# A's table on SyncE's queue, w0 indices in two reads, and the last stores cut differently in a low-rank-adapted residual kernel

## The chip, the cores and the metric

The kernel runs on one core of a Trainium2 chip. The metric is device microseconds of one execution, given as the median of several runs. Before the change it is 76.97 us (3 runs, 76.96 to 77.12). The engines are TensorE (PE), VectorE (DVE), ScalarE (ACT), GpSimd (POOL) and SyncE (SP), and 16 DMA engines move the data that the queues of SP, ACT and POOL issue.

## The reference, cut to what matters

```python
x = x + einsum('bct,bcd->bdt', x, L0_weights[cond])           # layer 0: 32 samples, 64x64 matrix each, picked from 200
H = einsum('btd,od->bto', x, W)                                # layer 1: 512 -> 512
xa = einsum('btd,brd->btr', x, A[adapter])                     # rank 16, picked from 8 adapters
delta = einsum('btr,bor->bto', xa, Bm[adapter]) * scalings[adapter][:, None, None]
out = x + H + delta
```

x is 32 samples of 64 x 512 in fp32.

## The kernel before, in words

Layer 1 works along the width and layer 0 along the channels, so the kernel multiplies by W plus the identity first (z), and applies layer 0, with the identity added to its matrices, to z afterwards. Two samples of 64 channels make one tile of 128 partitions, so there are 16 tiles (TILES = 16, 0 to 15). fp32 accuracy comes from splitting each operand in a high part (rounded to fp32r) and a low part (the difference), and adding three products; ACT makes the high parts and DVE the low ones. Tiles 0 and 1 (PLAIN = 2) are multiplied in plain fp32 instead, because they run before the split operands are there.

For a tile, PE computes z in two banks of 272 columns (`products`, L654; `plain_products`, L642, for tiles 0 and 1): the A part, which also holds the 32 columns of A (x times the adapter's A), and the W part. ACT and DVE take z out of PSUM in its high and low parts. `weigh_low_rank` (L688, L685) multiplies the low-rank columns by layer 0's matrix, `take_low_rank` (L540) and `low_of_low_rank` (L546) prepare them on DVE. `layer0` (L709, L710, L696, L714) then makes the output of the tile with four matmuls: two for z_high, one for the low-rank part with b, one for z_low. `take_out` (L413) copies it from PSUM to `out_sb` on ACT, and SP stores it.

All engines run a hand-written order and meet at semaphores. The PE order per tile is: A bank, two thirds of the W bank, layer 0 of the tile before, weigh_low_rank, last third of the W bank.

**The start.** The first transfers are index_sb, head_b, head_d and w_late on SP's queue (L241 to L244), and head_a, head_c and a_scales (A's table with the scalings, 260 KB) on ACT's (L327 to L329). SP then waits for the indices, reads those of layer 0's matrices of tiles 0 to 3 (8 values, `read_indices`), and issues the loads of these matrices (`load_w0`, L232, two DMAs of 16 KB a tile) with x of tile 3 between them (L228). From tile 4 on it reads four values at a time. POOL waits for a_scales (L306) before its first load of b (`load_b`, L290), then adds the identity to layer 0's matrices (`add_identity`, L299) and copies A's columns (`take_a`, L283), in this order: b of tiles 0 and 1, identity of tile 0, of tile 1, b of 2, A columns of 2, b of 3, identity of tiles 2 and 3, A columns of 3. ACT's `high_of_w0` (L400) and DVE's `low_of_w0` (L502) split layer 0's matrices of tiles 2 and 3 after that identity. On DVE `low_of_w0` stands ahead of `take_low_rank(2)` (L540).

**The end.** PE makes layer 0 of tile 14 whole (512 columns, `out_ps[0]`), then layer 0 of tile 15 in two parts: the A part (240 columns, `out_ps[1]`), then the W part (272 columns, a v_ps bank). ACT takes out tile 14 (L413), takes out tile 15's A part (L466) and issues its store (L469); SP stores tile 14 (L238); DVE takes out tile 15's W part (L629), and SP stores it (L265). ACT waits until all stores have landed (L471).

Of the kernel before, what the change touches and what calls it, by code (L numbers as in the profile page):

```python
# [6 lines left out]
def adapted_residual_kernel(nc, xt, heads, w0, head_a, head_b, head_c, head_d, w_late_t, a_t, b_t, out):  # L7
# [4 lines left out]
    ACT = mybir.ActivationFunctionType  # L12
# [5 lines left out]
    TILES = xt.shape[0] + EARLY  # L18
    C = w0.shape[1]
    PER = P // C  # L20
    K = WIDTH // P
    ADAPTERS, RANK, OUT = b_t.shape
# [9 lines left out]
    READ = 2  # L32
# [4 lines left out]
    AHEAD = 6  # L37
# [45 lines left out]
    with ctx:  # L83
# [6 lines left out]
        def sem(name):  # L90
            return ctx.enter_context(nc.semaphore(name))
# [9 lines left out]
        a_scales = sb("a_scales", [P, ADAPTERS * K * RANK + ADAPTERS], fp32)  # L101
# [19 lines left out]
        out_sb = sb("out_sb", [P, TILES, OUT], fp32)  # L121
# [9 lines left out]
        a_loaded = sem("a_loaded")  # L131
# [36 lines left out]
        z_low_ready = [sem("z_low_a_ready"), sem("z_low_w_ready")]  # L168
        out_done = sem("out_done")
        out_ready = sem("out_ready")  # L170
        last_done = sem("last_done")
        last_ready = sem("last_ready")
        stored = sem("stored")

# [30 lines left out]
        def read_indices(eng, kind, t, count, tiles):  # L205

            _, values = nc.values_load_multi_w_load_instructions(
                index_sb[0:1, PER * (TILES * kind + t):PER * (TILES * kind + t + tiles)], engines=(eng.engine,), min_val=0, max_val=count - 1)
            return [values[PER * i:PER * (i + 1)] for i in range(tiles)]
# [8 lines left out]
        def z_part(t, part):  # L218
            bank = bank_of(t, part)
            at, col, n = Z_PARTS[side(t)][bank]  # L220
            if t < PLAIN and part == A_PART and RAW_A[t] == 0:
                at += AC
            return z_ps[t % 2][:, bank, at:at + n], col, n

        @block.sync
        def _(sync):
            def load_x(t):
                sync.dma_start(x_raw[:, t - EARLY, :], xt[t - EARLY]).then_inc(x_loaded[t - 2], 16)  # L228

            def load_w0(which, t):  # L230
                for s in range(PER):
                    sync.dma_start(w0_sb[s * C:(s + 1) * C, t, s * C:(s + 1) * C],  # L232
                                   w0[ds(which[s], 1), :, :].rearrange("a c d -> (a c) d"),
                                   ).then_inc(w0_loaded[BATCH_OF[t]], 16)

            def store(t):
                sync.wait_ge(out_ready, t + 1)
                sync.dma_start(out[PER * t:PER * (t + 1), :, :].rearrange("s c l -> (s c) l"),  # L238
                               out_sb[:, t, :]).then_inc(stored, 16)

            sync.dma_start(index_sb[:], heads.rearrange("(a n) -> a n", a=1)).then_inc(index_loaded, 16)  # L241
            sync.dma_start(head[:, HEAD_AT[1]:HEAD_AT[2]], head_b).then_inc(head_loaded[1], 16)  # L242
            sync.dma_start(head[:, HEAD_AT[3]:HEAD_AT[4]], head_d).then_inc(head_loaded[3], 16)
            sync.dma_start(w_late[:, :, AC:AC + LATE], w_late_t).then_inc(w_late_loaded, 16)  # L244
            sync.wait_ge(index_loaded, 16)
            which = read_indices(sync, 0, 0, w0.shape[0], 2 * READ)
            sync.wait_ge(w0_cleared, 1)
            load_w0(which[0], 0)
            load_w0(which[1], 1)
            load_x(3)  # L250
            load_w0(which[2], 2)
            load_w0(which[3], 3)
            for t in range(4, TILES):
                if t % READ == 0:
                    which = read_indices(sync, 0, t, w0.shape[0], READ)
                load_x(t)
                load_w0(which[t % READ], t)
                if t >= AHEAD:
                    store(t - AHEAD)
            for t in range(TILES - AHEAD, TILES - 1):  # L260
                store(t)
            last = TILES - 1
            _, col, n = z_part(last, W_PART)
            sync.wait_ge(last_ready, 1)
            sync.dma_start(out[PER * last:, :, col:col + n].rearrange("s c l -> (s c) l"),  # L265
                           out_sb[:, last, col:col + n]).then_inc(stored, 16)

        @block.gpsimd
        def _(pool):
# [56 lines left out]
        def _(act):  # L326
            act.dma_start(head[:, HEAD_AT[0]:HEAD_AT[1]], head_a).then_inc(head_loaded[0], 16)  # L327
            act.dma_start(head[:, HEAD_AT[2]:HEAD_AT[3]], head_c).then_inc(head_loaded[2], 16)
            act.dma_start(a_scales[:], a_t).then_inc(a_loaded, 16)  # L329
            nc.scalar.activation(warmed[:], nc.const_aps.tensor(1.0, [1, 1], fp32), ACT.Copy)  # L330
            act.wait_ge(index_loaded, 16)
            first = read_indices(act, 1, 0, ADAPTERS, PLAIN)
# [78 lines left out]
            def take_out(t):  # L411
                act.wait_ge(out_done, t + 1)
                nc.scalar.activation(out_sb[:, t, :], out_ps[t % 2][:], ACT.Copy).then_inc(out_ready, 1)  # L413
# [31 lines left out]
            for t in range(3, last):  # L445
# [9 lines left out]
                if t % 2:  # L455
# [4 lines left out]
            high_of_z(last, A_PART)  # L460
            high_of_v(last)
            high_of_z(last, W_PART)
            take_out(last - 1)
            _, col, n = z_part(last, A_PART)
            act.wait_ge(out_done, last + 1)
            nc.scalar.activation(out_sb[:, last, col:col + n], out_ps[last % 2][:, 0:n],  # L466
                                 ACT.Copy).then_inc(out_ready, 1)
            act.wait_ge(out_ready, TILES)
            act.dma_start(out[PER * last:, :, col:col + n].rearrange("s c l -> (s c) l"),  # L469
                          out_sb[:, last, col:col + n]).then_inc(stored, 16)  # L470
            act.wait_ge(stored, 16 * (TILES + 1))  # L471

        @block.vector
        def _(dve):
# [149 lines left out]
            low_of_b(last)  # L624
            low_of_v(last)
            low_of_z(last, W_PART)
            _, col, n = z_part(last, W_PART)
            dve.wait_ge(last_done, 1)
            nc.vector.tensor_copy(out_sb[:, last, col:col + n], v_ps[(last + 1) % 2][:, 0:n]).then_inc(last_ready, 1)  # L629

        @block.tensor
        def _(pe):
# [72 lines left out]
            def layer0(t, dst, col, n, parts):  # L705
                pe.wait_ge(w0_low_ready, BATCH_OF[t] - BATCH_OF[PLAIN] + 1)
                for part in parts:
                    pe.wait_ge(z_high_ready[part], t - PLAIN + 1)
                nc.tensor.matmul(dst, w0_parts[:, t, 0, :], z_high[:, t % 2, col:col + n], start=True, stop=False)  # L709
                nc.tensor.matmul(dst, w0_parts[:, t, 1, :], z_high[:, t % 2, col:col + n], start=False, stop=False)  # L710
                add_low_rank(t, dst, col, n, False)
                for part in parts:
                    pe.wait_ge(z_low_ready[part], t - PLAIN + 1)
                return nc.tensor.matmul(dst, w0_parts[:, t, 0, :], z_low[:, t % 2, col:col + n], start=False, stop=True)  # L714

            def whole_layer0(t):
                pe.wait_ge(out_ready, t - 1)
                layer0(t, out_ps[t % 2][:], 0, OUT, (A_PART, W_PART)).then_inc(out_done, 1)
# [51 lines left out]
            w_bank(last, 0, 2 * K)  # L770
            weigh_low_rank(last)
            w_bank(last, 2 * K, 3 * K)
            whole_layer0(last - 1)
            pe.wait_ge(out_ready, last - 1)
            _, col, n = z_part(last, A_PART)
            layer0(last, out_ps[last % 2][:, 0:n], col, n, (A_PART,)).then_inc(out_done, 1)
# [52 lines left out]
```

## Time and profile before

| | |
|---|---|
| median of 3 runs | 76.97 us |
| the profiled execution's own time | 76.68 us |
| its span, first to last instruction | 75.0 us |
| granted TensorE clock | 1.000 of full speed in the mean |
| TensorE busy | 94% of the span |
| DVE, ACT, POOL busy | 74%, 68%, 44% |
| share of the chain that ended last | PE 86%, DMA 8% |
| DMA | 14.55 MB, mean 194 GB/s |

The times of the rows below are in microseconds from the span's start. A timeline row gives start, duration, engine, line, operation and what it writes and reads; in brackets stands how long the engine sat idle before it and what ended that. The chain of work that ended last is followed back from the last instruction and printed in order of time. In the names, SPq, ACTq and POOLq are the parts of these engines that issue DMAs. DMA queue q1 is SP's, q10 ACT's, q0 POOL's.

### The profile page before, as it was taken

To read this page: it belongs to the slowest core of one execution; us is meant where nothing else is said; L and a number is where in the kernel's file an instruction comes from. 1 tells how busy PE (TensorE), PEld (TensorE's weight loads), DVE (VectorE), ACT (ScalarE), POOL (GpSimd) and SP (SyncE) were. 2 spreads that over 40 slices of the span, in tenths; PEclk is the share of its full clock that TensorE was granted. 3 is DMA by queue.
4 is the path that set the end of the run, shared out by engine and by line. 5 is a ranking of instruction groups with operands and counts; after the bars stand their busy time and mean duration, and the time that the engine had idled before them with its cause. 6 is when DMAs were issued, how large, how long until landed. Compare 5 with 4: busy or idle time off the path is not lost.

```text
span 75.0 us, 1943 instructions
## 1 busy us (share of the span) xinstructions
PE 70.7 (94%) x468; PEld 65.4 (87%) x468; DVE 55.2 (74%) x143; ACT 51.3 (68%) x126; POOL 32.8 (44%) x76
## 2 busy tenths in 40 slices
PE   5999899999999999999999999999999999999940
PEld 5996689786999999999999999999999999999930
DVE  3019499897989877979797959797797949765920
ACT  0733888957988686977668666867696867566440
POOL 5700399997846282556245620690258320000000
PEclk9999999999999999999999999999999999999999
DMA  0999378786678757978968675578326430303025
GB/s 0 290 389 380 87 227 231 209 253 194 187 246 285 254 166 234 253 217 294 334 211 294 223 261 143 141 212 282 120 62 220 140 144 0 140 13 140 0 100 179
DMA packets 9677, 14.55 MB, mean 194 GB/s; under 512 B 3650, under 2 KB 4418, under 8 KB 9666
## 3 DMA queue, kind: packets, MB, share of 16 engines
q1 hardware_dynamic: 7554, 9.16, 37.5%
q0 software_dynamic: 1536, 4.20, 18.4%
q10 hardware_dynamic: 576, 1.07, 4.1%
q8 instruction: 4, 0.07, 0.4%
q14 instruction: 7, 0.06, 0.3%
HBM read 10.23 MB, written 4.19 MB: 192 GB/s over the span
## 4 chain that ended last, share of the span: by engine, by line
PE 86%; DMA 8%; SPq 1%; DVE 1%; issue 0%
PE z_ps L654 56%; DMA head<-head_d 8%; PE z_ps L642 6%; PE out_ps L696 5%; PE out_ps L709 4%; PE out_ps L710 4%; PE out_ps L714 4%; PE v_ps L688 2%; PE out_ps L702 2%; DVE out_sb L629 1%; PE v_ps L685 1%; SPq L242 0%; SPq L241 0%; PE v_ps L714 0%; PE v_ps L710 0%
## 5 line engine op out<-in xcount | busy, mean ns | idle before, releaser
L654 PE MATMUL z_ps<-moving,x_high 128*128 128x272 f32 x224 | 33.2, 288 | 0.0
L654 PEld LDWEIGHTS z_ps<-moving,x_high 128*128 128x128 f32 x224 | 29.8, 188 | 0.7 <-ACT z_plain L373 0.2
L290 POOL DMA_DIRECT2D b_raw<-b_t x32 | 16.2, 508 | 14.4 <-DMA a_scales<-a_t 5.4
L654 PE MATMUL z_ps<-moving,x_low 128*128 128x272 f32 x112 | 18.8, 289 | 0.0
L654 PEld LDWEIGHTS z_ps<-moving,x_low 128*128 128x128 f32 x112 | 15.8, 188 | 0.1
L511 DVE TENSOR_TENSOR z_low<-z_ps,z_high 128x272 fp32r<-128x272 f32 (+1 forms) x28 | 11.8, 422 | 1.2 <-ACT z_high L364 0.2
L283 POOL CAST moving<-a_table 128x128 fp32r x28 | 8.0, 316 | 10.5 <-PE z_ps L654 10.5
L520 DVE TENSOR_TENSOR b_stack<-b_raw,b_high 128x512 fp32r<-128x512 f32 x16 | 11.5, 718 | 0.4 <-ACT b_high L380 0.4
L380 ACT ACTIVATE b_high<-b_raw,group_sb 128x512 fp32r<-128x512 f32 x16 | 11.5, 716 | 0.0
L394 ACT ACTIVATE v_high<-v_ps,group_sb 128x128 fp32r<-128x128 f32 x16 | 5.9, 366 | 7.8 <-PE v_ps L688 7.8
L364 ACT ACTIVATE z_high<-z_ps 128x272 fp32r<-128x272 f32 (+1 forms) x28 | 10.5, 376 | 0.5 <-PE z_ps L654 0.3
L488 DVE TENSOR_TENSOR x_low<-x_raw,x_high 128x512 fp32r<-128x512 f32 x13 | 9.8, 757 | 0.1
L413 ACT ACTIVATE out_sb<-out_ps 128x512 f32<-128x512 f32 x15 | 8.8, 590 | 0.5 <-PE out_ps L714 0.5
L387 ACT ACTIVATE x_high<-x_raw 128x512 fp32r<-128x512 f32 x13 | 8.3, 637 | 0.0
L409 ACT ACTIVATE low_rank_parts<-own_low_rank 128x96 fp32r<-128x96 f32 x14 | 4.0, 284 | 5.9 <-DVE own_low_rank L540 5.9
L299 POOL TENSOR_TENSOR w_sb<-w_sb,ident 128x256 f32<-128x256 f32 (+1 forms) x9 | 6.9, 769 | 2.5 <-DMA w_sb<-w 2.4
L696 PE MATMUL out_ps<-b_stack,v_stack 128*128 128x512 f32 (+1 forms) x16 | 7.0, 435 | 0.0
L546 DVE TENSOR_TENSOR low_rank_parts<-own_low_rank,low_rank_parts 128x32 fp32r<-128x32 f32 x14 | 3.2, 227 | 4.9 <-ACT low_rank_parts L409 4.9
L709 PE MATMUL out_ps<-z_high,w_parts 128*128 128x512 f32 (+1 forms) x14 | 5.4, 388 | 0.0
L710 PE MATMUL out_ps<-z_high,w_parts 128*128 128x512 f32 (+1 forms) x14 | 5.4, 383 | 0.0
L714 PE MATMUL out_ps<-z_low,w_parts 128*128 128x512 f32 (+1 forms) x14 | 5.4, 382 | 0.0
L560 DVE SCALAR_TENSOR_TENSOR v_stack<-v_ps,group_sb,v_rest 128x128 fp32r<-128x128 f32 x14 | 4.9, 351 | 0.5
(58 smaller groups left out, 77.1 us busy)
## 6 DMA issues: line engine op xcount, KB each, us to landing
b_raw<-b_t POOLq DMA_DIRECT2D x32, 128.0 KB, 3.2
out<-out_sb SPq DMA_DIRECT2D x15, 256.0 KB, 3.2
x_raw<-xt SPq DMA_DIRECT2D x13, 256.0 KB, 3.7
w_sb<-w SPq DMA_DIRECT2D x32, 16.0 KB, 3.2
w_late<-w_late_t SPq DMA_DIRECT2D x1, 480.0 KB, 6.9
head<-head_c ACTq DMA_DIRECT2D x1, 400.0 KB, 4.2
head<-head_d SPq DMA_DIRECT2D x1, 384.0 KB, 6.1
head<-head_a ACTq DMA_DIRECT2D x1, 264.0 KB, 2.9
```

What stands on the lines that cost most here:

```text
L290: pool.dma_start(b_raw[s * C:(s + 1) * C, t % BBUFS, :], b_t[ds(which[s], 1), :, :].rearrange("a r (g n) -> (a r) g n", g=1) .to_broadcast ...
L364: nc.scalar.activation(z_high[:, t % 2, col:col + n], z, ACT.Copy).then_inc(z_high_ready[part], 1)
L380: nc.scalar.activation(b_high[:, t % 2, :], b_raw[:, t % BBUFS, :], ACT.Copy, scale=group_sb[:, LOW_B:LOW_B + 1]).then_inc(b_high_ready, 1)
L413: nc.scalar.activation(out_sb[:, t, :], out_ps[t % 2][:], ACT.Copy).then_inc(out_ready, 1)
L488: nc.vector.tensor_tensor(out=x_low[:, t % XBUFS, :], in0=x_of(t), in1=x_high[:, t % XBUFS, :].bitcast(fp32), op=ALU.subtract).then_inc(x_ ...
L511: nc.vector.tensor_tensor(out=z_low[:, t % 2, col:col + n], in0=z, in1=z_high[:, t % 2, col:col + n].bitcast(fp32), op=ALU.subtract).then_ ...
L520: nc.vector.tensor_tensor(out=b_stack[:, t % 2, :], in0=b_raw[:, t % BBUFS, :], in1=b_high[:, t % 2, :].bitcast(fp32), op=ALU.subtract).th ...
L654: last = nc.tensor.matmul(z_bank(t, part), x[:, t % XBUFS, k * P:(k + 1) * P], moving[:, int(n == HL), k, at:at + HALF], start=((n, k) == ...
L696: return nc.tensor.matmul(dst, v_stack[:, t % 2, :], b_stack[:, t % 2, col:col + n], start=False, stop=stop)
L709: nc.tensor.matmul(dst, w0_parts[:, t, 0, :], z_high[:, t % 2, col:col + n], start=True, stop=False)
L710: nc.tensor.matmul(dst, w0_parts[:, t, 1, :], z_high[:, t % 2, col:col + n], start=False, stop=False)
L714: return nc.tensor.matmul(dst, w0_parts[:, t, 0, :], z_low[:, t % 2, col:col + n], start=False, stop=True)
```

## The change

Four edits:

1. The load of a_scales moves from ACT's queue (third there) to SP's, between head_d and w_late.
2. The indices of layer 0's matrices for tiles 0 to 3 are read in two steps of four values instead of one of eight: the second step stands after x of tile 3 is issued.
3. Layer 0 of tile 14 is computed in two halves of 256 columns, the first into `out_ps`, the second into tile 14's own z bank, which is free by then. ACT takes each half out as it is done, and SP stores each by itself.
4. Of tile 15, DVE takes out the A part and SP stores it; ACT takes out the W part, the last one, and issues its store itself.

```diff
+            sync.dma_start(a_scales[:], a_t).then_inc(a_loaded, 16)
             sync.dma_start(w_late[:, :, AC:AC + LATE], w_late_t).then_inc(w_late_loaded, 16)
             sync.wait_ge(index_loaded, 16)
-            which = read_indices(sync, 0, 0, w0.shape[0], 2 * READ)
+            which = read_indices(sync, 0, 0, w0.shape[0], READ)
             sync.wait_ge(w0_cleared, 1)
             load_w0(which[0], 0)
             load_w0(which[1], 1)
             load_x(3)
-            load_w0(which[2], 2)
-            load_w0(which[3], 3)
+            which = read_indices(sync, 0, READ, w0.shape[0], READ)
+            load_w0(which[0], 2)
+            load_w0(which[1], 3)
...
-            _, col, n = z_part(last, W_PART)
-            sync.wait_ge(last_ready, 1)
-            sync.dma_start(out[PER * last:, :, col:col + n].rearrange("s c l -> (s c) l"),
-                           out_sb[:, last, col:col + n]).then_inc(stored, 16)
+            sync.wait_ge(half_ready, 1)
+            store_columns(last - 1, 0, OUT // 2)
+            sync.wait_ge(out_ready, last)
+            store_columns(last - 1, OUT // 2, OUT // 2)
+            _, col, n = z_part(last, A_PART)
+            sync.wait_ge(first_ready, 1)
+            store_columns(last, col, n)
...
-            act.dma_start(a_scales[:], a_t).then_inc(a_loaded, 16)
...
-            take_out(last - 1)
-            _, col, n = z_part(last, A_PART)
-            act.wait_ge(out_done, last + 1)
-            nc.scalar.activation(out_sb[:, last, col:col + n], out_ps[last % 2][:, 0:n],
+            act.wait_ge(half_done, 1)
+            nc.scalar.activation(out_sb[:, last - 1, 0:OUT // 2], out_ps[(last - 1) % 2][:, 0:OUT // 2],
+                                 ACT.Copy).then_inc(half_ready, 1)
+            act.wait_ge(out_done, last)
+            nc.scalar.activation(out_sb[:, last - 1, OUT // 2:], z_ps[(last - 1) % 2][:, 0, 0:OUT // 2],
                                  ACT.Copy).then_inc(out_ready, 1)
-            act.wait_ge(out_ready, TILES)
+            _, col, n = z_part(last, W_PART)
+            act.wait_ge(last_done, 1)
+            nc.scalar.activation(out_sb[:, last, col:col + n], v_ps[(last + 1) % 2][:, 0:n],
+                                 ACT.Copy).then_inc(last_ready, 1)
+            act.wait_ge(last_ready, 1)
             act.dma_start(out[PER * last:, :, col:col + n].rearrange("s c l -> (s c) l"),
                           out_sb[:, last, col:col + n]).then_inc(stored, 16)
...
-            _, col, n = z_part(last, W_PART)
-            dve.wait_ge(last_done, 1)
-            nc.vector.tensor_copy(out_sb[:, last, col:col + n], v_ps[(last + 1) % 2][:, 0:n]).then_inc(last_ready, 1)
+            _, col, n = z_part(last, A_PART)
+            dve.wait_ge(out_done, last + 1)
+            nc.vector.tensor_copy(out_sb[:, last, col:col + n], out_ps[last % 2][:, 0:n]).then_inc(first_ready, 1)
...
-            whole_layer0(last - 1)
+            pe.wait_ge(out_ready, last - 2)
+            layer0(last - 1, out_ps[(last - 1) % 2][:, 0:OUT // 2], 0, OUT // 2,
+                   (A_PART, W_PART)).then_inc(half_done, 1)
+            layer0(last - 1, z_ps[(last - 1) % 2][:, 0, 0:OUT // 2], OUT // 2, OUT // 2,
+                   (A_PART, W_PART)).then_inc(out_done, 1)
```

## Rows read from the trace of the kernel before

**Rows 1.** The chain in order of time: start, us, what
```profile
1.71 6.11 DMA head<-head_d
...
70.21 0.23 PE out_ps L709
...
71.14 0.11 PE out_ps L709
...
71.96 0.14 PE v_ps L714
...
72.12 0.44 DVE out_sb L629
```
**Rows 2.** Timeline of ACT and SP from 65 us on
```profile
71.18 0.60 ACT L413 ACTIVATE out_sb<-out_ps 128x512 f32<-128x512 f32 x1 [0.53 <-PE out_ps L714]
71.67 0.36 ACT L466 ACTIVATE out_sb<-out_ps 128x240 f32<-128x240 f32 x1
72.06 0.36 ACTq L469 DMA_DIRECT2D out<-out_sb  x1
...
72.59 0.33 SPq L265 DMA_DIRECT2D out<-out_sb  x1
```
**Rows 3.** DMA issues, us to landing: tile 13 (66 to 70 us), then tile 15's stores
```profile
out<-out_sb SPq DMA_DIRECT2D x1, 256.0 KB, 2.0
...
out<-out_sb SPq DMA_DIRECT2D x1, 136.0 KB, 2.0
out<-out_sb ACTq DMA_DIRECT2D x1, 120.0 KB, 2.2
```
**Rows 4.** DMA traffic in 73:73.3, 73.3:73.6 and 73.6:73.9 us, one row each
```profile
DMA packets 54, 0.11 MB, mean 369 GB/s; under 512 B 0, under 2 KB 0, under 8 KB 54
...
q10 hardware_dynamic: 83, 0.08, 81.6%
...
DMA packets 113, 0.10 MB, mean 333 GB/s; under 512 B 16, under 2 KB 113, under 8 KB 113
```
**Rows 5.** Start: issues to landing, ACT's issue of a_scales, q10 in 6.0:6.5 and 7.0:7.5
```profile
w_late<-w_late_t SPq DMA_DIRECT2D x1, 480.0 KB, 6.9
...
a_scales<-a_t ACTq DMA_DIRECT2D x1, 260.0 KB, 6.2
...
1.79 0.45 ACTq L329 DMA_DIRECT2D a_scales<-a_t  x1
...
q10 hardware_dynamic: 69, 0.13, 68.6%
...
q10 hardware_dynamic: 3, 0.00, 2.2%
```
**Rows 6.** Timelines of PE, POOL, ACT, DVE and PE's weight loads, 8 to 19 us
```profile
9.42 2.00 PE L642 MATMUL z_ps<-w_late,head 128*128 128x272 f32 x8
...
8.77 2.27 POOL L290 DMA_DIRECT2D b_raw<-b_t  x4 [5.41 <-DMA a_scales<-a_t]
...
14.90 1.06 POOL L299 TENSOR_TENSOR w_sb<-w_sb,ident 128x256 f32<-128x256 f32 x1
...
16.00 0.42 ACT L400 ACTIVATE w_parts<-w_sb 128x256 fp32r<-128x256 f32 x1 [0.82 <-POOL w_sb L299]
...
16.91 0.41 DVE L502 TENSOR_TENSOR w_parts<-w_sb,w_parts 128x256 fp32r<-128x256 f32 x1
17.33 0.19 DVE L540 TENSOR_TENSOR own_low_rank<-z_ps,own_rank 128x32 f32<-128x32 f32 x1
...
18.14 0.19 PEld L688 LDWEIGHTS v_ps<-w_parts,low_rank_parts 128*128 128x128 f32 x1 [0.39 <-DVE low_rank_parts L546]
```
**Rows 7.** SP's queue, 2 to 12 us; then landing of its last w0 issue of tile 3
```profile
2.18 0.67 SPq L244 DMA_DIRECT2D w_late<-w_late_t  x1
...
9.42 2.44 SPq L232 DMA_DIRECT2D w_sb<-w  x4
...
w_sb<-w SPq DMA_DIRECT2D x1, 16.0 KB, 3.3
```

More of the change, by code:

```diff
@@ L170, in adapted_residual_kernel @@
         out_ready = sem("out_ready")
+        half_done = sem("half_done")
+        half_ready = sem("half_ready")
         last_done = sem("last_done")
+        first_ready = sem("first_ready")
         last_ready = sem("last_ready")
@@ L259, in _, with store_columns @@
                     store(t - AHEAD)
-            for t in range(TILES - AHEAD, TILES - 1):
+            last = TILES - 1
+            for t in range(TILES - AHEAD, last - 1):
                 store(t)
-            last = TILES - 1
-            _, col, n = z_part(last, W_PART)
-            sync.wait_ge(last_ready, 1)
-            sync.dma_start(out[PER * last:, :, col:col + n].rearrange("s c l -> (s c) l"),
-                           out_sb[:, last, col:col + n]).then_inc(stored, 16)
+            def store_columns(t, col, n):
+                sync.dma_start(out[PER * t:PER * (t + 1), :, col:col + n].rearrange("s c l -> (s c) l"),
+                               out_sb[:, t, col:col + n]).then_inc(stored, 16)
+            sync.wait_ge(half_ready, 1)
[5 more added lines that the diff above has]
+            store_columns(last, col, n)
         @block.gpsimd
@@ L462, in _ @@
             high_of_z(last, W_PART)
-            take_out(last - 1)
-            _, col, n = z_part(last, A_PART)
-            act.wait_ge(out_done, last + 1)
-            nc.scalar.activation(out_sb[:, last, col:col + n], out_ps[last % 2][:, 0:n],
-                                 ACT.Copy).then_inc(out_ready, 1)
-            act.wait_ge(out_ready, TILES)
+            act.wait_ge(half_done, 1)
[3 more added lines that the diff above has]
+            nc.scalar.activation(out_sb[:, last - 1, OUT // 2:], z_ps[(last - 1) % 2][:, 0, 0:OUT // 2],
+                                 ACT.Copy).then_inc(out_ready, 1)
+            _, col, n = z_part(last, W_PART)
[3 more added lines that the diff above has]
+            act.wait_ge(last_ready, 1)
             act.dma_start(out[PER * last:, :, col:col + n].rearrange("s c l -> (s c) l"),
                           out_sb[:, last, col:col + n]).then_inc(stored, 16)
-            act.wait_ge(stored, 16 * (TILES + 1))
+            act.wait_ge(stored, 16 * (TILES + 2))
         @block.vector
```

## The prediction

> **What bounds the kernel now.** I read the chain that ended last first, in order of time. It begins with the landing of head_d at 1.71 + 6.11 = 7.82 us, runs through TensorE's matmuls without a gap worth naming up to 72.10 us, and leaves by DVE's copy of tile 15's W part, 72.12 + 0.44 = 72.56 us [rows 1]. So the kernel is TensorE's work plus a head and a tail, and an edit can win only in these two. The middle is touched only if the head lets TensorE begin it earlier.
>
> The tail next. SP issues the last store at 72.59 us [rows 2], it lands 2.0 us later [rows 3], at 74.59, and the span ends at 75.0: 0.4 us of closing work. Three stores are in flight there: tile 14's 256 KB, issued when ACT's copy of it is done (71.18 + 0.60 = 71.78), 120 KB issued by ACT at 72.06, 136 KB by SP at 72.59 [rows 2]. The reader is to see that they queue. Tile 13's 256 KB, with nothing beside it, took 2.0 us from issue to landing; the last store, with half the bytes, took 2.0 us too, and ACT's, still smaller, 2.2 [rows 3]. ACT's queue moves most of its bytes between 73.3 and 73.6 us, over 1.2 us after its issue at 72.06 [rows 2, 4].
>
> The head last. PE starts tile 0's A bank at 9.42 us; w_late, which it needs, lands at 2.18 + 6.9 = 9.08 [rows 5 to 7]. Behind that stands a second chain, which shares nothing with PE's. a_scales is issued on ACT's queue at 1.79 and lands 6.2 us later, at 7.99 [rows 5]. POOL, which had waited 5.41 us for it, starts its first b load at 8.77 and adds the identity to tiles 2 and 3 from 14.90 to 15.96 [rows 6]. ACT waits 0.82 us for this and splits these matrices at 16.00. DVE takes their low part at 16.91 to 17.32, starts `take_low_rank(2)` at 17.33, and PE's weight load for `weigh_low_rank(2)`, idle for 0.39 us, starts at 18.14 upon it [rows 6]. Whatever PE wins before 18.14 is lost there unless POOL is earlier too. This is the most important reading for the head.
>
> **The tail, part by part.** Tile 14 in halves: four matmuls of 512 columns take 4 x 0.23 us, those of 240 columns 0.11 each [rows 1], in proportion. Eight of 256 columns cost 8 x 0.115 = 0.92 us, what four cost now; the four extra weight loads are hidden as they are in tile 15's parts. Bounds: 0 to +0.1 us; I take 0. PE begins tile 14 at 70.21, so the first half is done at 70.67 and the second at 71.13. ACT's copies took 0.60 us for 512 columns and 0.36 for 240 [rows 2], so 0.37 for 256: 70.71 to 71.08 and 71.17 to 71.54. SP issues at 71.11 and 71.57. The A part leaves PE at 71.14 + 4 x 0.11 = 71.58. DVE's copy took 0.44 us for 272 columns [rows 1], so about 0.42 for 240, and SP issues at 72.05. SP is idle before each of these issues; an issue takes 0.33 us there [rows 2], so none stands in another's way. The W part leaves PE at 72.10. ACT copies 272 columns in 0.36 to 0.44 us (its own 240, DVE's 272), I take 0.40, and issues at 72.55 to 72.58, against 72.59 now: the hand-over itself wins 0.02 us.
>
> What wins is the queue. With 2 KB rows the engines moved 369 GB/s, with rows of about 1 KB 333 [rows 4]. Tile 13's 0.262 MB took 0.71 us of its 2.0 by the first rate, so 1.29 us are fixed. A half of tile 14 (0.131 MB) then moves in 0.39 us, the A part in 0.37, the W part (0.139 MB) in 0.42. The issues are 0.46, 0.48 and 0.52 us apart, each more than the transfer before it needs, so nothing is left in the queue when the last begins. It lands 1.29 + 0.42 = 1.71 us after 72.57, at 74.28, where it was 74.59: -0.31 us. Bounds: -0.40 if the small stores also move at the higher rate and the copy is at its short end, +0.18 if a store issued by ACT needs 2.2 us here too.
>
> The Trainium skill speaks against this edit: "DMA: Bandwidth & Descriptors" gives, under "Anatomy of one DMA", a fit of about 2.0 us plus bytes / 436 GB/s, and under "Rules for kernel authors" it wants small transfers joined. By that fit, an estimate from the page for another issue path, the last store would need 2.32 us and land at 74.89, and the sum would be +0.30. The trace disagrees: tile 13's store needed 2.0 us where the fit gives 2.60.
>
> **The head, part by part.** a_scales on SP's queue: its issue takes the place of w_late's, 2.18 in place of 1.79, but its bytes move far later, most of them around 6.0 to 6.5, and the last three packets after 7.0 [rows 5]. The order of issue, a, b, c, d, a_scales, w_late, stays what it was. head_d no longer shares with it and may land up to 0.5 us earlier; but PE then waits for w_late, whose bytes stand behind the same sum as before and which lands at 9.08. PE could start at about 9.25 in place of 9.42 (-0.17 at most), which the wait at 18.14 takes back. What counts is a_scales' own landing: -0.1 us if it no longer gives way to anything, +1.09 if it shares with w_late up to the end of that. I take 0, near the row of its last packets: behind head_d on one queue the same bytes stand ahead of it.
>
> SP's queue: the reads are eight values as before, but four of them move past the loads for tiles 0 and 1 and x of tile 3, which therefore go out earlier. Nobody waits for these three: POOL adds these identities after its b loads. The matrices of tiles 2 and 3 stand behind the same work as before and one more issue, 0.45 us on ACT's queue [rows 5], so they go to 9.42 + 0.45. Their last issue starts at 11.86 - 0.47 = 11.39 now and lands 3.3 us later, at 14.69 [rows 7]; POOL takes it up at 14.90. The cover is 0.21 us, and 0.45 would use it up: +0.24 us on POOL's chain if the landing keeps its 3.3 us. Against it, x of tile 3 (256 KB) is further out of the way by then. Bounds 0 to +0.24; I take 0, since the load that slowed these landings is reduced. ACT's queue loses one issue and gains nothing from it: it next waits for DVE. I give the whole head -0.02 us, for shifted overlaps.
>
> **The sum.** 0 - 0.31 - 0.02 = -0.33 us. The profiled execution took 76.68 us (75.0 of span, 1.68 around it), so it becomes 76.35. The median of the runs shown lies 0.29 above it: 76.97 - 0.33 = 76.64 us. About 0.2%, 0.15 us, is what a measurement of this kernel can tell from none.
>
> **The rivals.**
> - **a_scales lands late (slower).** Everything of its queue, w_late and the early matrix loads too, shares with it. POOL's chain has no slack, so each 0.1 us goes to the end. From +0.48 us on the tail's gain is used up and the kernel slower; at w_late's landing it is 1.09 - 0.31, 77.75 us. For it: the issue is 0.39 later and three queue neighbours are new. Against it: its bytes never moved before 5.5 us, and w_late's came behind. 0.10.
> - **The head takes back what the tail gives (same).** a_scales is later by its issue, 0.39, or the matrices by 0.24: 76.88 to 77.03 us. 0.13.
> - **The tail's queue is no bound (same).** If landing and not moving makes the 2.0 us, only the hand-over's 0.02 is won: 76.95 us. For it: all three sizes landed in 2.0 to 2.2 us. Against it: rows 4 show ACT's bytes held up. 0.10.
> - **A store issued by ACT needs 2.2 us (slower).** 72.57 + 2.2 = 74.77, +0.18: 77.15 us. The skill's fit, above, goes this way. 0.05.
> - **POOL's chain gets shorter (faster).** Its identity adds run beside DVE's work; with DVE earlier by 0.2 to 0.4 us and a_scales by 0.1, up to 0.25 more is won, of which PE can use 0.17: 76.4 us. 0.14.
>
> **How the numbers follow.** The forecast, 76.5 to 76.8 us, has 0.48. Faster: 0.48 + 0.14 = 0.62; same 0.13 + 0.10 = 0.23; slower 0.10 + 0.05 = 0.15. The range reaches from 76.3, the faster rival, to 77.1, past the two that end at no change; it leaves out the slow ones.
>
> **What would show it.** In the profile of the changed kernel: ACT's half copies at about 70.7 and 71.2, the last issue on ACT's queue at 72.57 if the head is unchanged, landing in about 1.7 us; POOL's first b load still near 8.8, its add for tiles 2 and 3 near 14.9, and the weight load of `weigh_low_rank(2)` near 18.1. PE starts tile 0's A bank at about 9.25. The prediction is wrong if POOL's first b load moves by over 0.2 us, or if the last store needs 2 us.

## The result, and the profile after

The changed kernel takes 77.39 us in the median of 20 runs (76.59 to 78.09); the kernel before, timed beside it, 76.97 (20 runs, 76.32 to 77.60). The ratio is 1.0057, 95% interval 1.0033 to 1.0080: slower by about 0.44 us, where 0.33 us less was forecast. Two later timings of the unaltered kernel gave 1.0042 and 1.0064. The ratios, here and below, leave out the executions over 1.5% slower than the fastest of their kernel; the medians take in all.

The first profiled execution of the changed kernel was its slowest one, 78.09 us with a span of 76.4. I read it beside a second profile of the same kernel (77.10 us, span 75.4), and count as the change's doing only what both show.

The end first. The changed kernel: the last piece of the chain, ACT's issue of the last store, and the stores' times from issue to landing (70 to 77 us).

```profile
72.93 0.40 ACT out_sb L483
...
73.35 0.36 ACTq L486 DMA_DIRECT2D out<-out_sb  x1
...
out<-out_sb SPq DMA_DIRECT2D x2, 128.0 KB, 1.7
out<-out_sb ACTq DMA_DIRECT2D x1, 136.0 KB, 2.7
out<-out_sb SPq DMA_DIRECT2D x1, 120.0 KB, 1.8
```

Three of four stores land 1.7 to 1.8 us after their issue, as forecast; they answer to [rows 3], 2.0 and 2.2. The last one, the one that counts, needs 2.7. From the start of the last copy to the end of the span it is 76.4 - 72.93 = 3.5 us, before 75.0 - 72.12 = 2.9 [rows 1]. Why, its DMA traffic from 74 to 76 us shows, in 40 steps of 0.05 us:

```profile
GB/s 365 288 154 116 85 174 283 348 348 348 348 348 240 87 186 0 0 0 0 0 22 22 22 22 0 22 22 0 44 0 0 0 0 0 0 0 0 0 0 0
...
q10 hardware_dynamic: 144, 0.14, 20.2%
...
q14 instruction: 1, 0.01, 1.0%
```

The store moves at 348 GB/s until 74.6 us and is all but through at 74.7. There one packet of kind instruction, on queue q14, is served; its 1.0% of 16 engines' 2 us is 0.32 us. For that long next to nothing else starts, and then 22 GB/s move until 75.45, a sixteenth of 348, what one of 16 DMA engines carries. The packets of q10 from 74.8 to 75.6 us:

```profile
q10 hardware_dynamic: 9, 0.01, 4.0%
```

The store has 144 packets, and nine are again a sixteenth: one engine's whole share moves behind the instruction packet. The second profile shows the same nine, with the packet at 73.7 us, 1.32 us behind the store's issue (1.37 here), and the store at 2.6 us. Which engine serves a packet the trace doesn't say. The kernel before has such a packet too, but at 76 us, after its span, and its tail in [rows 4] has none.

The head of the changed kernel, in the views of [rows 5 to 7]: landings, then the timelines of PE, POOL, PE's weight loads and SP.

```profile
w_late<-w_late_t SPq DMA_DIRECT2D x1, 480.0 KB, 6.1
...
a_scales<-a_t SPq DMA_DIRECT2D x1, 260.0 KB, 5.2
...
9.88 2.00 PE L659 MATMUL z_ps<-w_late,head 128*128 128x272 f32 x8
...
8.15 2.26 POOL L303 DMA_DIRECT2D b_raw<-b_t  x4 [4.79 <-DMA a_scales<-a_t]
...
13.21 0.53 POOL L296 CAST moving<-a_table 128x128 fp32r x2 [0.52 <-DVE a_table L607]
...
15.03 0.74 POOL L312 TENSOR_TENSOR w_sb<-w_sb,ident 128x256 f32<-128x256 f32 x1
...
18.66 0.19 PEld L705 LDWEIGHTS v_ps<-w_parts,low_rank_parts 128*128 128x128 f32 x1 [0.46 <-DVE low_rank_parts L563]
...
10.02 2.44 SPq L235 DMA_DIRECT2D w_sb<-w  x4
```

a_scales is issued at 2.18 and lands at 7.38, 0.61 us earlier than in [rows 5]; POOL starts its b loads at 8.15, not 8.77. But the identity add of tiles 2 and 3 starts at 15.03, no earlier than the 14.90 of [rows 6], and PE starts tile 0's A bank at 9.88, not 9.42. In the second profile the same steps read:

```profile
8.94 2.00 PE L659 MATMUL z_ps<-w_late,head 128*128 128x272 f32 x8
...
14.98 0.83 POOL L312 TENSOR_TENSOR w_sb<-w_sb,ident 128x256 f32<-128x256 f32 x1 [0.43 <-DMA w_sb<-w]
...
18.00 0.19 PEld L705 LDWEIGHTS v_ps<-w_parts,low_rank_parts 128*128 128x128 f32 x1 [0.39 <-DVE low_rank_parts L563]
```

Two things differ. PE's start at 9.88 or 8.94 is no property of the kernel, since it is the same one. And POOL's add waits 0.43 us for layer 0's matrices in the second profile and not at all in the first. What both have is a wait before it: POOL comes to its copy of A's columns of tile 2 earlier, finds `a_table`, which DVE finishes from a_scales' data, not ready, and waits 0.52 us (0.54 in the second profile, 0.61 in a third, and none in the kernel before). Another 0.20 us pass before its next b loads. That uses up the 0.61 us by which a_scales was earlier. The 9.88 comes from TensorE's first passes. PE's busy time and instructions from 4.5 to 7 us, the kernel before, then the changed one:

```profile
4.50:7.00 2.50, 2.50 (x12) 1.00 1.02 375
```
```profile
4.50:7.00 2.50, 2.50 (x7) 1.00 1.04 400
```

The granted clock reads 1.00 (2.4 GHz) in both, but the same passes start 0.23 us apart in the one and 0.46 in the other, as at 1.2 GHz, until about 6.7 us. PE had been busy with its warm-up matmuls before in both. Over the profiles of the two kernels and of all experiments this window holds 7 to 12 passes, in kernels with a_scales moved and not moved: 7 and 11 in the two profiles of the changed kernel above, 8 with edits 3 and 4 alone. With 7 or 8 passes the weight load at 18 us comes at 18.4 to 18.9, with 11 or 12 at 17.5 to 18.2. It is chance of the execution, worth up to 0.9 us at PE's start. The Trainium skill agrees in kind ("TensorE: Matmul & The Clock Gate", Part 1: the gate runs freely and doesn't start anew with the kernel); the spread here is wider than the 500 ns either way that it gives for the transition.

### The profile page after: what moved, and what is told of

Its sections match the earlier page's. It is cut to its first block, busy times and chain, and to the rows that moved or that the text cites. A ratio compares the mean times of both kernels' runs of the same rounds, so it can differ in the third digit from the quotient of the medians.

```text
span 76.4 us, 1957 instructions
## 1 busy us (share of the span) xinstructions
PE 72.0 (94%) x472; PEld 66.4 (87%) x472; DVE 55.7 (73%) x143; ACT 51.6 (68%) x127; POOL 33.4 (44%) x76
## 4 chain that ended last, share of the span: by engine, by line
PE 94%; ACT 1%; issue 0%
PE z_ps L671 55%; PE z_ps L659 11%; PE v_ps L740 5%; PE out_ps L713 5%; PE out_ps L726 4%; PE out_ps L727 4%; PE out_ps L731 4%; PE v_ps L705 3%; PE out_ps L719 2%; PE v_ps L702 1%; ACT out_sb L483 1%; PE v_ps L731 0%; PE v_ps L713 0%; PE v_ps L726 0%; PE v_ps L727 0%; PE z_ps L726 0%
## 5 line engine op out<-in xcount | busy, mean ns | idle before, releaser
L537 DVE TENSOR_TENSOR b_stack<-b_raw,b_high 128x512 fp32r<-128x512 f32 x16 | 12.1, 759 | 0.4 <-ACT b_high L392 0.4
L425 ACT ACTIVATE out_sb<-out_ps 128x512 f32<-128x512 f32 x14 | 8.3, 590 | 0.0
L713 PE MATMUL out_ps<-b_stack,v_stack 128*128 128x512 f32 (+2 forms) x16 | 6.9, 429 | 0.0
L726 PE MATMUL out_ps<-z_high,w_parts 128*128 128x512 f32 (+2 forms) x14 | 5.3, 379 | 0.0
L727 PE MATMUL out_ps<-z_high,w_parts 128*128 128x512 f32 (+2 forms) x14 | 5.3, 375 | 0.0
L731 PE MATMUL out_ps<-z_low,w_parts 128*128 128x512 f32 (+2 forms) x14 | 5.2, 374 | 0.0
```

The costliest lines, as they stand in the source:

```text
L537: nc.vector.tensor_tensor(out=b_stack[:, t % 2, :], in0=b_raw[:, t % BBUFS, :], in1=b_high[:, t % 2, :].bitcast(fp32), op=ALU.subtract).th ...
L713: return nc.tensor.matmul(dst, v_stack[:, t % 2, :], b_stack[:, t % 2, col:col + n], start=False, stop=stop)
```

## The experiments

All ran beside the kernel before on the same chip, 12 runs each; the ratio is to it. "Packet" is when the last packet of q14 moves, "store" the us from issue to landing of the last store, "weights" the start of PE's weight load for `weigh_low_rank(2)`, "medians" those of this kernel and of the kernel before in us.

| label | edits | packet | store | weights | ratio (95%) | medians |
|---|---|---|---|---|---|---|
| e1_after_again | 1 2 3 4 | 73.7 | 2.6 | 18.00 | 1.0042 (1.0000 to 1.0084) | 77.16, 76.75 |
| e2_head_only | 1 2 | 74.5 | 2.0 | 18.57 | 1.0003 (0.9969 to 1.0037) | 76.88, 76.75 |
| e3_tail_only | 3 4 | 76.1 | 1.8 | 18.39 | 0.9943 (0.9900 to 0.9985) | 76.70, 76.75 |
| e4_table_only | 1 | 76.1 | 2.0 | 18.23 | 1.0038 (0.9992 to 1.0084) | 76.94, 76.75 |
| e5_table_and_tail | 1 3 4 | 74.7 | 2.0 | 18.81 | 1.0027 (0.9982 to 1.0073) | 77.36, 76.86 |
| e6_reads_and_tail | 2 3 4 | 73.6 | 2.1 | 17.76 | 0.9982 (0.9939 to 1.0025) | 76.59, 76.86 |
| e7_tail_padded | 3 4, 8 waits | 72.7 | 2.3 | 18.29 | 1.0005 (0.9961 to 1.0048) | 77.33, 76.86 |
| e8_after_padded | 1 2 3 4, 24 waits | 69.1 | 1.8 | 18.20 | 0.9962 (0.9925 to 1.0000) | 76.48, 76.86 |
| e9_reads_tail_padded | 2 3 4, 24 waits | 69.7 | 1.8 | 18.59 | 0.9959 (0.9918 to 1.0000) | 76.47, 76.89 |
| e10_tail_padded24 | 3 4, 24 waits | 69.5 | 1.8 | 18.53 | 0.9928 (0.9889 to 0.9967) | 76.54, 76.89 |
| e11_reads_only | 2 | 75.9 | 2.0 | 17.96 | 0.9987 (0.9953 to 1.0021) | 76.79, 76.89 |
| e12_halves_only | 3 | 75.5 | 1.8 | 17.71 | 0.9915 (0.9875 to 0.9956) | 76.29, 76.89 |
| e13_after_third | 1 2 3 4 | 74.7 | 2.7 | 18.88 | 1.0064 (1.0025 to 1.0103) | 77.25, 76.80 |
| e14_after_padded8 | 1 2 3 4, 8 waits | 69.2 | 1.8 | 18.41 | 0.9988 (0.9952 to 1.0023) | 76.65, 76.80 |
| e15_after_padded40 | 1 2 3 4, 40 waits | 69.8 | 1.8 | 18.81 | 0.9996 (0.9960 to 1.0031) | 76.65, 76.80 |
| e16_after_sent_by_sp | 1 2 3 4, SP sends all | 73.3 | 2.1 | 18.04 | 1.0044 (1.0009 to 1.0080) | 76.99, 76.80 |
| e17_halves_table_padded | 1 3, 24 waits | 68.9 | 1.8 | 18.05 | 1.0028 (0.9994 to 1.0063) | 76.76, 76.70 |
| e18_halves_padded | 3, 24 waits | 68.7 | 1.8 | 17.50 | 0.9958 (0.9921 to 0.9995) | 76.19, 76.70 |

e1 to e4 ran side by side on one chip, and so did e5 to e8, e9 to e12, e13 to e16, and e17 with e18.

### Which half of the change loses

e1 is the changed kernel unaltered.

> The changed kernel, unaltered, beside the kernel before. In its first profile the head had cost 0.45 us (tile 0's A bank at 9.88 us, not 9.42, after TensorE's first passes ran 0.46 us apart, not 0.23) and the last store needed 2.7 us, not 1.7, with one instruction packet of a DMA queue beside it. Theory head: the slow first passes belong to the change and show again, ratio 1.005 to 1.008. Theory tail: the head's delay was chance (A bank at 9.25 to 9.45), the 2.7 us of the last store shows again, ratio 1.003 to 1.008. Theory chance: both are gone in this profile, ratio 0.994 to 1.001.

e2 is the kernel before with the head edits:

```diff
+            sync.dma_start(a_scales[:], a_t).then_inc(a_loaded, 16)
             sync.dma_start(w_late[:, :, AC:AC + LATE], w_late_t).then_inc(w_late_loaded, 16)
-            which = read_indices(sync, 0, 0, w0.shape[0], 2 * READ)
+            which = read_indices(sync, 0, 0, w0.shape[0], READ)
...
+            which = read_indices(sync, 0, READ, w0.shape[0], READ)
...
-            act.dma_start(a_scales[:], a_t).then_inc(a_loaded, 16)
```

> The kernel before with edits 1 and 2 alone (a_scales on SyncE's queue, indices in two reads). Theory head: it carries the loss, 0.3 to 0.6 us, ratio 1.004 to 1.008, with tile 0's A bank at 9.7 us or later. Theory tail: the head edits change nothing, ratio 0.998 to 1.002, A bank at 9.25 to 9.45 and the weight load of weigh_low_rank(2) near 18.1.

e3 is the changed kernel with these lines set back, e4 the kernel before with the move of a_scales alone.

> The kernel before with edits 3 and 4 alone (tile 14 in halves, last part taken out and sent by ScalarE). Theory head: the tail gains what was forecast, ratio 0.994 to 0.998, the last store landing 1.7 us after its issue at about 72.6. Theory tail: the last store needs 2.4 to 2.8 us, with an instruction packet beside it at 74 to 75 us, ratio 1.003 to 1.007.

> The kernel before with edit 1 alone (a_scales on SyncE's queue, ahead of w_late). Theory head by the queue: the move alone carries the head's loss, ratio 1.004 to 1.008, as edits 1 and 2 together. Theory head by the reads: the move is free, ratio 0.998 to 1.002, and the loss needs edit 2. Theory tail: 0.998 to 1.002 as well, and edits 1 and 2 together also show no loss.

The parts don't add up. By the ratios the tail edits alone gain 0.57% (76.75 x 0.0057 = 0.44 us; the medians show less, 76.70 beside 76.75), the head edits alone neither gain nor lose, and together they lose 0.42%. (e4, the move alone, stands at 1.0038; in its profile POOL waits 0.69 us for tile 1's matrices, whose group goes out at 6.61 us. It comes back below.) So the theory "head" falls for the last store, and the theory "tail" falls as it stood: with edits 3 and 4 alone that store takes 1.8 us, where 1.7 were forecast, and the packet is at 76 us. e3's timeline and landings, and the q14 row of 76 to 77 us:

```profile
72.50 0.40 ACT L482 ACTIVATE out_sb<-v_ps 128x272 f32<-128x272 f32 x1 [0.56 <-PE v_ps L730]
...
out<-out_sb ACTq DMA_DIRECT2D x1, 136.0 KB, 1.8
...
q14 instruction: 1, 0.01, 3.3%
```

From the last copy's start to the span's end it is 75.1 - 72.50 = 2.6 us. So something joins the halves: the head edits lengthen SP's program by a DMA and a second load of index values, and the last packet of q14 comes 2 us earlier.

### Is it the place of the instruction packet

e5 takes the second read out of the changed kernel, e6 the move of a_scales.

> The changed kernel with the indices read in one step of eight again (edits 1, 3 and 4). Theory code position: SyncE's program length before its last store decides when its last instruction packet is fetched. If the move alone is enough, the packet is still at 73.5 to 75 us inside the last store, which needs 2.6 us, ratio 1.000 to 1.006; if it needs the second read, the packet comes after 76 us, the store needs 1.7 to 1.8 us, ratio 0.992 to 0.998. Theory transfers: the last store is slow whenever a_scales is on SyncE's queue and the tail is cut; it needs 2.6 us here whatever the packet does. Head: first b load near 8.1 us, second identity add waiting for w0 as with edit 1 alone.

> The changed kernel with a_scales on ScalarE's queue again (edits 2, 3 and 4). Theory code position: the second read adds instructions to SyncE's program, so the packet is at 73.5 to 75 us and the last store needs 2.6 us, ratio 1.001 to 1.006. Theory transfers (it needs a_scales on SyncE's queue): the last store needs 1.8 us, ratio 0.993 to 0.997.

In both the packet was back at 73.5 to 75 us, so either edit moves it. But the store needed 2.0 and 2.1 us, not 2.6, which neither theory had. The packet's distance from the last store's issue is nearly the same, 1.39 and 1.40 us in e5 and e6 and 1.32 to 1.37 in the three profiles of the changed kernel, but the order is not. In the changed kernel nine packets of the store come behind it; in e5 and e6 it is served as the store's own packets end. e5's DMA traffic from 74.7 to 75.6 us:

```profile
DMA packets 0, 0.00 MB, mean 0 GB/s; under 512 B 0, under 2 KB 0, under 8 KB 0
```

So a share of the store that moves behind the packet goes with 0.8 to 0.9 us more, and a packet just at the end of the bytes with 0.2 to 0.3 us more. What decides the order no row shows. With no packet there the last store needs 1.8 us, in e3, e8 to e10, e12, e14, e15, e17 and e18. Where tile 14 is stored whole it needs 2.0, in the kernel before, e4 and e11, and in e2 too, with the packet at 74.5 us.

e7, e8 and later kernels add waits that are met long before, which compute and move nothing, where SP idles:

```diff
+            for _ in range(24):
+                sync.wait_ge(index_loaded, 16)
             sync.wait_ge(half_ready, 1)
             store_columns(last - 1, 0, OUT // 2)
```

> Edits 3 and 4 alone (0.9943 without padding) with eight waits that are already met added to SyncE's program ahead of the first half store, where SyncE idles. They compute and move nothing. Theory code position: the last instruction packet is fetched earlier than in the unpadded one (after 76 us), and if it lands at 73 to 74.5 us the last store needs 2.6 us and the ratio is 1.000 to 1.006; if eight are too many it is fetched before 72.5 us and the ratio stays 0.990 to 0.998. Theory transfers: packet and store stay as in the unpadded kernel, 1.8 us, ratio 0.990 to 0.998.

> The changed kernel (1.0042 and 1.0057) with 24 waits that are already met added to SyncE's program ahead of the first half store. Theory code position: the last instruction packet is fetched while SyncE idles, before 72 us, the last store needs 1.7 to 1.8 us instead of 2.6, and the ratio falls by 0.8 us to 0.992 to 0.997. Theory transfers: the store still needs 2.6 us, ratio 1.003 to 1.007.

Eight idle waits in the kernel of e3 brought the packet from 76 into the first stores at 72.7 us, the last store to 2.3 us, and the ratio from 0.9943 to 1.0005 (the intervals overlap; the last copy's start to the span's end grew from 2.6 to 3.2 us). Twenty-four in the changed kernel brought it to 69 us, in front of all stores, the last store to 1.8, and the ratio to 0.9962. These two in opposite directions are what no theory of transfers explains.

> Edits 2, 3 and 4 with 24 met waits on SyncE ahead of the first half store. Code position: packet before 72 us, last store 1.8 us, ratio 0.991 to 0.997. Reads: in the one profile so far of edits 2, 3 and 4, head_d landed at 6.7 us and a_scales at 7.1, as early as with a_scales moved; if the second read does this, they land at 6.5 to 7.2 us again, and if that was chance, at 7.8 to 8.2 as in the kernel before.

e9 had the packet at 69.7 us, the last store at 1.8, a_scales, not moved, at 1.79 + 5.4 = 7.2 us, and the ratio 0.9959. The early landing of e6 was there again, without the move.

> Edits 3 and 4 alone with 24 met waits (eight gave 1.0005, none 0.9943). Code position: 24 bring the packet to before 71 us, clear of the stores; last store 1.8 us, ratio 0.991 to 0.997. If the padding costs by itself (more waits in SyncE's path), more of it is worse: 1.002 or above, whatever the packet does.

e10 shows that padding isn't what costs: 24 waits gave 0.9928 where eight gave 1.0005. Then side by side on one chip, with the unaltered kernel as the standard:

> The changed kernel unaltered, as the standard of this call. Code position: packet at 73.5 to 75 us, about 1.4 us after SyncE's last issue, last store 2.3 to 2.7 us, ratio 1.003 to 1.007. Chance: last store 1.8 us in this profile, ratio under 1.002.

> The changed kernel with eight met waits ahead of the first half store. Code position: the packet comes earlier than in the unpadded kernel but may still meet one of the four stores (72 to 73 us, as eight did with edits 3 and 4 alone, where the last store needed 2.3 us), ratio between those of the other two, 0.998 to 1.003. Chance: as the unpadded one.

> The changed kernel with 40 met waits there (24 gave 0.9962, packet at 69 us). Code position: packet before 70 us, last store 1.8 us, ratio 0.993 to 0.998, 0.6 to 0.8 us under the unpadded one of this call. If padding costs, or if chance made the 24-wait result: ratio 1.002 or above.

e13 lost 0.64% with its store at 2.7 us; e14 and e15, the same kernel with idle waits, stood at 0.9988 and 0.9996. In medians it is 77.25 against 76.65 and 76.65 us: the packet's place is worth 0.60 us (in the profiles the last store takes 0.9 us more). e14's place was not as expected, 69 us and not 72 to 73; its time was. The row of its last copy, of the last store's landing, and of q14 from 69 to 70 us (75.0 - 72.41 = 2.6 us again):

```profile
72.41 0.40 ACT L485 ACTIVATE out_sb<-v_ps 128x272 f32<-128x272 f32 x1 [0.56 <-PE v_ps L733]
...
out<-out_sb ACTq DMA_DIRECT2D x1, 136.0 KB, 1.8
...
q14 instruction: 1, 0.01, 3.0%
```

e16 leaves ACT's copy and lets SP issue the last store too:

```diff
             sync.wait_ge(first_ready, 1)
             store_columns(last, col, n)
+            _, col, n = z_part(last, W_PART)
+            sync.wait_ge(last_ready, 1)
+            store_columns(last, col, n)
...
-            act.dma_start(out[PER * last:, :, col:col + n].rearrange("s c l -> (s c) l"),
-                          out_sb[:, last, col:col + n]).then_inc(stored, 16)
```

> The changed kernel, with the last part taken out by ScalarE as there but stored by SyncE. No padding. Code position: the packet is fetched after SyncE's last issue, which is now that of the last store, so it comes behind the store's bytes or after the span, the store needs 1.7 to 1.9 us, ratio 0.993 to 0.998. Theory sender: the same, and then the padded kernels of this call must be slow. Theory head (the loss sits in edits 1 and 2): ratio stays 1.002 or above.

This missed. The packet came at 73.3 us, 0.6 us behind SP's last issue but still ahead of the last store's bytes, the store needed 2.1 us, and the kernel stayed slow at 1.0044. And the store was issued late. ACT's last copy, and SP's issue (72.6 to 72.8 us):

```profile
72.04 0.40 ACT L486 ACTIVATE out_sb<-v_ps 128x272 f32<-128x272 f32 x1 [0.56 <-PE v_ps L731]
...
72.71 0.33 SPq L270 DMA_DIRECT2D out<-out_sb  x1
```

The copy ends at 72.44 and the issue comes 0.27 us later, where all other kernels need 0.02 to 0.03 for this step; what held SP no row names. From the last copy's start to the span's end it is 75.2 - 72.04 = 3.2 us, 0.6 more than in e14. That covers the whole distance of 1.0044 from e14's 0.9988 (0.43 us), so the third expectation, a loss in the head, finds no support here. The sender is not the cause, and my picture that a packet behind SP's last issue is harmless was wrong.

### What the tail is worth, and what the head costs

> The kernel before with edit 2 alone. If the second read makes the first transfers land early: head_d at 6.5 to 7.0 us, a_scales at 7.0 to 7.4, POOL's first b load at 7.8 to 8.1, ratio 0.995 to 1.000. If that was chance: 7.8 and 8.0 us, POOL at 8.7 to 9.0, ratio 0.999 to 1.002. The last store is SyncE's and is not met by a packet in either.

The last store and the packet behaved as written, the landings too, and so early landings need no move of a_scales: head_d at 6.6 and a_scales at 7.3 us. e12 has edit 3 alone:

> Edit 3 alone: tile 14 in halves, each stored by SyncE; tile 15's parts as in the kernel before, the last one taken out by VectorE and stored by SyncE. Theory queue: nothing waits in front of the last store, it lands 1.7 to 1.8 us after its issue instead of 2.0, and ScalarE's 1.7 to 1.8 instead of 2.2; ratio 0.994 to 0.998, most of the gain of edits 3 and 4. Theory sender: the gain of edits 3 and 4 comes from ScalarE sending the last part; here ratio 0.999 to 1.001 and 2.0 us.

```profile
out<-out_sb SPq DMA_DIRECT2D x2, 128.0 KB, 1.7
out<-out_sb SPq DMA_DIRECT2D x1, 136.0 KB, 1.8
out<-out_sb ACTq DMA_DIRECT2D x1, 120.0 KB, 1.8
```

All four stores (e12's landings, 70 to 80 us) need 1.7 to 1.8 us, with the last part copied by VectorE and sent by SP: the halves take the queue away, and who copies and sends the last part is worth nothing that shows (from the last copy's start to the span's end 2.6 us in e12 as in e3). 0.9915 is more than the tail's 0.3 us; part of it may be chance, as e18 with the same edit gave 0.9958. In e12 a_scales, not moved, landed at 1.79 + 5.4 = 7.2 us. So the 7.99 of [rows 5] was one of two cases of the old order, and the worse: 8.0 to 8.2 in the kernel before, e3 and e7, 7.1 to 7.4 in e6, e9, e10, e11, e12 and e18. With the move it was 7.1 to 8.0.

The last pair differs in the move alone, with the packet clear of the stores.

```diff
-            act.dma_start(a_scales[:], a_t).then_inc(a_loaded, 16)
+            sync.dma_start(a_scales[:], a_t).then_inc(a_loaded, 16)
```

> Edits 1 and 3 with 24 met waits (edit 4 left out, so the last store is VectorE's and SyncE's as in the kernel before). If the move of a_scales costs: 0.2 to 0.3 us above the kernel beside it, ratio 0.995 to 0.999, the weight load of weigh_low_rank(2) later than 18.2 us. If the move is free: the same ratio as beside it, 0.990 to 0.995. The last store lands 1.8 us after its issue in either, the instruction packet at 69 to 71 us.

> Edit 3 alone with 24 met waits: the standard for the kernel beside it, and a check that edit 3 alone (0.9915 unpadded) owes its time to the queue of stores and not to where its packet fell. Expected: ratio 0.990 to 0.995, last store 1.8 us, packet at 69 to 71 us. If the padding costs: 0.996 or above.

e17, with the move: SP's second group of matrices, POOL's identity adds of tile 1 and of tiles 2 and 3, and PE's weight load.

```profile
9.90 2.44 SPq L235 DMA_DIRECT2D w_sb<-w  x4
...
11.51 0.74 POOL L313 TENSOR_TENSOR w_sb<-w_sb,ident 128x128 f32<-128x128 f32 x1 [0.87 <-DMA w_sb<-w]
...
15.21 0.76 POOL L313 TENSOR_TENSOR w_sb<-w_sb,ident 128x256 f32<-128x256 f32 x1
...
18.05 0.19 PEld L706 LDWEIGHTS v_ps<-w_parts,low_rank_parts 128*128 128x128 f32 x1 [0.81 <-DVE low_rank_parts L564]
```

e18, without it:

```profile
9.43 2.44 SPq L235 DMA_DIRECT2D w_sb<-w  x4
...
14.60 0.76 POOL L312 TENSOR_TENSOR w_sb<-w_sb,ident 128x256 f32<-128x256 f32 x1 [0.68 <-DMA w_sb<-w]
...
17.50 0.19 PEld L706 LDWEIGHTS v_ps<-w_parts,low_rank_parts 128*128 128x128 f32 x1 [0.40 <-DVE low_rank_parts L564]
```

Ratios 1.0028 and 0.9958, medians 76.76 and 76.19: the move costs 0.57 us here, and the weight loads stand 0.55 us apart (the spans of these two executions only 0.3, 74.7 and 74.4). Both kernels had a_scales by 7.4 us (e17 2.18 + 4.9, e18 1.79 + 5.6). Once a_scales is early, POOL waits for layer 0's matrices, in e17 0.87 us for those of tile 1 and then no more, in e18 0.68 for those of tiles 2 and 3. They stand behind the moved issue on SP's queue: the first group at 6.61, not 6.13, the second at 9.90, not 9.43.

With the second read the wait at tile 1 goes away, as its first group goes out at 5.4 us. POOL then waits 0.51 to 0.61 us for DVE's `a_table`, in all three profiles of the changed kernel and in e6, e8, e9, e11 and e15 (and in e5, without the second read). Its second group still goes out at 10.02, and e1 waits 0.43 us for it. There the move costs nothing that can be told from noise: 1.0003 against 0.9987 (e2, e11), and 0.9962 against 0.9959 (e8, e9, with the packet clear of the stores).

## Why the prediction was wrong, point by point

- **The tail's sum held where no packet was in the way.** Issue to landing was forecast at 1.71 us and is 1.8 wherever no packet is in the way; ACT's copy was forecast at 0.40 and is 0.40; the queue was gone. From the last copy to the end of the span it is 2.6 us against 2.9, that is the 0.3 of the sum. The halves alone bring it.
- **The step that failed first: "It lands 1.29 + 0.42 = 1.71 us after 72.57".** I priced the last store by rows in which nothing but stores moved, and did not ask what else runs on the DMA engines there. An instruction packet at 76 us, one step behind the end of the kernel before, came to 73.7 and 74.7 when SP's program had become longer. A store is through when its last engine is, and nine of its 144 packets, one engine's, moved behind the instruction packet and took it from 1.8 to 2.7 us. With the packet moved away by idle waits 0.60 us of median time were gone, twice. That the packet holds the engine up fits the order of the packets, and also e5 and e6, where none of the store's is behind it and 0.2 to 0.3 us are lost; no row names the engine. The Trainium skill has both halves of it: "Runtime: NRT & Kernel Launch", Instruction fetch mechanics, says that each engine's instruction memory is refilled by a DMA queue of its own, ahead of execution; "DMA: Bandwidth & Descriptors", in the section on why a DMA increments its semaphore by 16, that only the full count means that all data has landed. The traces agree: 22 GB/s, one engine, for 0.5 us after the bulk. By what rule a packet falls on a time no run here settles.
- **The step that failed second: "The cover is 0.21 us, and 0.45 would use it up", and behind it "I take 0, since the load that slowed these landings is reduced."** The move's issue on SP's queue was priced at +0.24 us at most, against POOL's chain bound by a_scales. With an early a_scales that chain is bound by something else. Without edit 2 it is the matrices, and there is no cover: POOL waits for them 0.64 and 0.68 us in e12 and e18, without the move, and 0.69 and 0.87 in e4 and e17, with it, and the move costs 0.57 us in the cleanest pair. In the changed kernel it is first DVE's `a_table`, 0.52 to 0.61 us in its three profiles, which the prediction doesn't have at all, and the matrices only in one of the three (e1, 0.43 us); their second group went out at 10.02, not 9.87. So a_scales' early landing won nothing in these profiles (the add of tiles 2 and 3 at 14.92 to 15.03, before 14.90) and the move costs at most some 0.1 us (the two pairs above). The rival "the head takes back what the tail gives" had the wait for the matrices, as did the sentence on the cover; I gave it 0.13.
- **"I take 0" for a_scales' landing was wrong in the other direction and didn't matter.** It landed at 7.38, not 7.99, but kernels that don't move it reach 7.1 to 7.4 as well. One profile showed one of two cases and I took it as the kernel.
- **PE before 18.14 us.** That the wait there takes back what PE wins held: 8.94 against 9.42 at the A bank became 18.00 against 18.14. That PE could win 0.17 us at most did not: w_late was to land at 9.08 as before, and landed at 2.66 + 6.0 = 8.7 there. When TensorE's first passes are slow, its lateness shows at the weight load too (9.88 and 18.66).
- **The rule against small stores.** The fit of the Trainium skill ("DMA: Bandwidth & Descriptors", Anatomy of one DMA) wanted 2.32 us for the last store, an estimate from it for another issue path; undisturbed it took 1.8. That the store took 2.6 in the changed kernel is not this rule's doing, since e8, e14 and e15 have the same stores.
- **The parts together.** The tail gives -0.26 us by the rows (2.90 to 2.64 us from the last copy's start to the span's end), the packet +0.60 by the medians (e13, e14, e15). The changed kernel with the packet away, 0.9982 in the mean of e8, e14 and e15, is 0.14 us under the kernel before and not 0.26, which leaves some 0.1 us for the head. The sum is some +0.45 us, and the first timing says +0.44. The ratios of the tail edits alone, 0.9943 and 0.9928 (e3, e10), would give the tail more than its rows do, e3's medians less; the intervals, 0.4% either way, don't settle it.

The version that beats both kernels is edit 3 alone: 0.9915 (0.9875 to 0.9956), 76.29 us beside 76.89; with padding 0.9958 (0.9921 to 0.9995), 76.19 beside 76.70.

## What to carry to other kernels

Ask of the last store, whose slowest DMA engine ends the kernel, what else the engines serve in its 2 us, and look in the DMA rows for packets of kind instruction shortly behind the end: a few instructions more in a queue's program can bring one in. Before costing a step against a wait, look at who is second behind the waited one (here DVE's table, then the matrices), and take a second profile: here a_scales' landing and TensorE's first passes differed between executions by more than the effect that was forecast. And when two halves of a change measure -0.6% and 0.0% apart but +0.4% together, look for what they share besides data, here the length of one engine's program.

## What the runs showed of the hardware that was not expected

- Idle waits move time: eight in a place where SP had nothing to do lengthened the tail by 0.5 us (e3 to e7; 0.6% by the ratios, whose intervals overlap), and eight or 24 gained 0.8% in the changed kernel (e13 to e14, e1 to e8).
- TensorE's passes of one shape ran 0.46 us apart up to 6.7 us after the start in one execution and 0.23 apart from 5.5 us on in another of the same kernel (e1), with the granted clock at 1.00 in the rows of both.
- The first transfers landed in two patterns in kernels with the same order of issue: a_scales at 8.0 to 8.2 us, or at 7.1 to 7.4. Of the kernels without edits 1 and 2 three had the late one and three the early one; with edit 2 alone of the two it was always the early one; with the move all between 7.1 and 8.0 occurred. Why was not found.
- One instruction packet of 0.01 MB near the end of a 136 KB store went with 0.2 to 0.3 us more for it when it was served as the store's packets ended (e5, e6), and with 0.8 to 0.9 when nine of the store's 144 packets were left (the changed kernel, in three profiles), at nearly the same distance from the issue.
